# Two cross-attention stages: float32r scores on half-array row pairs, other rings of banks, transferred tail rows, and scores three steps ahead

## The reference

```
# first cross-attention: 16 heads of 16 features, 1024 context rows, a mask
qh = split(q @ wq.T + bq);  kh = split(k @ wk.T + bk);  vh = split(v @ wv.T + bv)
scores = where(mask == 0, -1e9, einsum('bhqd,bhkd->bhqk', qh, kh) / 4)
out = (softmax(scores) @ vh) @ wo.T + bo
# second: one key/value head of 16 features for all 16 query heads, 512 memory rows that are
# chosen first, row by row, by an argmax over the context
logits = einsum('bhld,bmd->bhlm', qh, mk) / 4
out = (softmax(logits) @ mv) @ Wc.T
```

## Time and profile before

| | |
|---|---|
| median of 3 timed runs | 982.57 us |
| the profiled execution, its own time | 984.73 us |
| its span, first to last instruction | 982.3 us |
| mean granted TensorE clock | 0.961 |
| PE busy, share of the span | 889.5 us, 91% |
| DVE busy | 668.3 us, 68% |
| ACT busy | 500.9 us, 51% |
| first cross-attention, first score to last values | 152.9 to 379.8 us |
| second cross-attention, the same | 716.9 to 845.9 us |

### The profile page before, as it was taken

How to read it: one execution, slowest core, us unless ns; L and a number is a source line. 1 busy time by engine, 2 the same in 40 slices (tenths; PEclk the granted TensorE clock), 3 DMA queues, 4 the chain that set the end, 5 groups by cost and what they waited for, 6 DMA issues and landing times. The chain is left out here.

```text
span 982.3 us, 13451 instructions
## 1 busy us (share of the span) xinstructions
PE 889.5 (91%) x4332; PEld 488.0 (50%) x4332; DVE 668.3 (68%) x1371; ACT 500.9 (51%) x996; POOL 334.9 (34%) x340
## 2 busy tenths in 40 slices
PE   5889988999999998599999999998989999769996
PEld 2445553433333324366667888787433322534575
DVE  4865667888889944435558776875699896455654
ACT  3786544677777773012126656563207778243321
POOL 7335636400000001136557666563420000125833
PEclk9999998999999999699989999999998999959999
DMA  5030017122212810753240000000200550075200
GB/s 157 1 139 22 1 31 117 24 51 51 48 43 53 297 54 1 261 232 126 87 129 1 1 1 1 1 1 1 81 3 20 194 196 1 1 281 181 70 17 27
DMA packets 41656, 73.81 MB, mean 75 GB/s; under 512 B 8964, under 2 KB 27780, under 8 KB 40436
## 3 DMA queue, kind: packets, MB, share of 16 engines
q1 hardware_dynamic: 36372, 59.68, 19.9%
q0 software_dynamic: 4400, 13.11, 4.3%
q10 hardware_dynamic: 816, 0.17, 0.1%
HBM read 49.67 MB, written 10.49 MB: 61 GB/s over the span
## 5 line engine op out<-in xcount | busy, mean ns | idle before, releaser
L1081 DVE TENSOR_REDUCE c_amx<-PS 128x1 f32<-128x512 f32 x256 | 159.1, 683 | 27.5 <-PE PS L981 27.1
L1174 ACT ACTIVATE c_aE<-PS 128x512 f32<-128x512 f32 x256 | 132.6, 602 | 47.1 <-PE PS L993 46.9
L1881 POOL TENSOR_SCALAR s_Pn<-s_Pr,s_rs 128x512 f32<-128x512 f32 x64 | 100.4, 1569 | 55.7 <-DVE s_rs L1923 55.6
L72 POOL TENSOR_SCALAR rstd<-mv 128x4 f32<-128x4 f32 x8 | 1.9, 234 | 336.6 <-DVE mv L95 336.6
L981 PE MATMUL PS<-c_aKs,c_aQs 99*128 99x512 bf16 x256 | 96.4, 387 | 5.1 <-DMA c_aQs<-area 3.6
L993 PE MATMUL PS<-c_aQs,c_aKs 99*128 99x512 bf16 x256 | 94.5, 380 | 3.5 <-ACT c_aE L1174 2.3
L1081 DVE TENSOR_REDUCE h_amx<-PS 128x1 f32<-128x512 f32 x128 | 79.5, 682 | 8.7 <-PE PS L981 8.3
L1174 ACT ACTIVATE h_aE<-PS 128x512 f32<-128x512 f32 x128 | 67.6, 600 | 21.6 <-PE PS L993 21.3
L2019 ACT ACTIVATE s_Pr<-PS,s_nmx 128x512 f32<-128x512 f32 x64 | 44.2, 690 | 65.5 <-DVE s_nmx L1916 65.5
L1004 PE MATMUL PS<-c_aE,c_VB 128*17 128x512 f32 x512 | 67.4, 598 | 0.1
L981 PEld LDWEIGHTS PS<-c_aKs,c_aQs 99*128 99x128 bf16 x256 | 24.9, 98 | 79.0 <-DVE c_amx L1081 55.4
(11 more groups left out here) (486 smaller groups left out, 1969.7 us busy)
## 6 DMA issues: line engine op xcount, KB each, us to landing
area<-in_e_w SPq DMA_DIRECT2D x16, 512.0 KB, 10.1
area<-in_g_w SPq DMA_DIRECT2D x8, 1024.0 KB, 6.3
c_aKs<-area SPq DMA_DIRECT2D x48, 128.0 KB
g_B<-in_g_b SPq DMA_DIRECT2D x1, 4096.0 KB, 14.1
c_aQs<-area SPq DMA_DIRECT2D x48, 64.0 KB
h_aQs<-h_QP SPq DMA_DIRECT2D x48, 64.0 KB
early<-in_ctxT SPq DMA_DIRECT2D x2, 1024.0 KB, 7.6
e_B<-in_e_b SPq DMA_DIRECT2D x1, 2048.0 KB
```

The source lines that it names most:

```text
L1081: dve.tensor_reduce(self.mx[:, qt, j, half:half + 1], PS[:, n % MB, :], AX.X, ALU.max).then_inc(self.max_done, 1)
L1174: act.activation(self.E[kt % 2][:, j, :], PS[:, MB + x % XB, :], ACT.Exp, scale=0.25).then_inc(self.exp_done, 1)
L1881: pool.tensor_scalar(Pn[g % NPB][:, :], Pr[g % NPB][:, :], rs[:, g % NPB:g % NPB + 1], None, ALU.mult).then_inc(pn_ready, 1)
```

## The change

**Operands.** Queries and keys are split into two float32r parts in place of three bf16 ones. Three blocks of 16 rows do (`NBLK` = 3), with the three tail rows ahead of them: 51 rows. They stand twice, for even heads from partition 0, for odd heads from partition 64 (`rows_of_head`), so that a product uses one half of the array's rows. The two matrices of a step's pair always use opposite halves: the second pass takes heads in the order 1, 0, 3, 2 (`x ^ 1`). The copies and subtractions that made the third part, on ScalarE, VectorE and GpSimd, go away. Bytes per unit are nearly the same: 102 rows of 2 x 1024 float32 against 99 of 4 x 1024 bf16.

**Banks.** The maxima rotate over four banks and the exponentials over three; there is no bank for transposes alone. The transposed maxima take a turn in the exponentials' ring, the transposed output one in the maxima's (`special_item`, `out_item`).

**Tail rows.** ScalarE copies the transposed maxima once, all 128 partitions, into `MTs` (`copy_maxima`), and SP sends three rows to each of four heads (`tails`). The transposes stand three steps ahead of the unit's end.

**Scores three steps ahead** (`AHEAD` = 3) and so 11 in place of 9 steps' scores ahead of the first stage's first step, 7 in place of 5 in the second.

**Loads.** SP's queue first fetches the constant query tails once into the chip (`load_tail`), and then sends them, two transfers for each unit. The second mixture's experts are loaded from ScalarE's queue, in units 1 to 4 at steps 0 and 2.

The core of the diff:

```diff
-NBLK = 6
+NBLK = 3
-MB, XB = 3, 3
+MB, XB, VALUE_BANK = 4, 3, 6
+AHEAD = 3
...
-        self.Qs = [sb(f"Qs{n}", [ROWS, GH, S], BF16) for n in range(NQ)]
-        self.Ks = [sb(f"Ks{n}", [ROWS, KH, NK], BF16) for n in range(NKB)]
+        self.Qs = [sb(f"Qs{n}", [P, PAIRS_H, S], F32R) for n in range(NQ)]
+        self.Ks = [sb(f"Ks{n}", [P, self.KP, NK], F32R) for n in range(NKB)]
...
-        n = (u + 1) * self.C + kt + 1
+        n = (u + 1) * self.C + kt + AHEAD
...
+        for u in range(UNITS):
+            self.tails(sp, u)
+            if u + 2 < UNITS:
+                if u >= 1:
+                    sp.wait_ge(self.av_done, u * self.KT)
+                load(u + 2, (u + 2) % 3)
+
+    def tails(self, sp, u):
+
+        sp.wait_ge(self.t_copied, u + 1)
+        for j in range(GH):
+            sp.dma_start(self.Qs[u % self.NQ][tail_of_head(j), j // 2, :].bitcast(F32),
+                         self.MTs[32 * j:32 * j + TAIL_ROWS, :].bitcast(F32)).then_inc(self.tails_in, 16)
...
+            item = self.max_item(u, c, j)
+            self.wait_max_bank(pe, item)
+            r = rows_of_head(j)
+            pe.matmul(self.max_bank(item), self.Qs[u % self.NQ][r, j // 2, qt * P:(qt + 1) * P],
+                      self.Ks[self.key_buffer(u)][r, j // 2 % self.KP, half * BANK:(half + 1) * BANK],
                       start=True, stop=True).then_inc(self.s_done, 1)
...
+            j = x ^ 1
+            r = rows_of_head(j)
+            if kt == 0 and x == 0:
+                pe.wait_ge(self.tails_in, 16 * GH * (u + 1))
...
-                if kt == KT - 1 and u + 1 < UNITS:
...
+                if kt == KT - AHEAD and u + 1 < UNITS:
                     maxima_transposes(u + 1)
...
-        for c in range(C + 1):
+        for c in range(C + AHEAD):
...
-        def tails(u):
+        def copy_maxima(u):
             act.wait_ge(self.mT_done, u + 1)
-            for j in range(GH // 2):
-                act.activation(self.Qs[u % self.NQ][TAIL:ROWS, j, :],
-                               PS[32 * j:32 * j + TAIL_ROWS, 7, :].bitcast(BF16)[:, 0:S],
-                               ACT.Copy).then_inc(self.q_ready, 1)
+            if u > 0:
+                act.wait_ge(self.tails_in, 16 * GH * u)
+            act.activation(self.MTs[:, :], self.exp_bank(self.special_item("m", u)).bitcast(BF16)[:, 0:S],
+                           ACT.Copy).then_inc(self.t_copied, 1)
...
-KEY_SLOTS = ((0, 3, 5), (1, 4), (2,))
-QUERY_SLOTS = ((0, 1, 2), (3, 4), (5,))
+KEY_SLOTS = ((0, 1), (2,))
+QUERY_SLOTS = ((0, 2), (1,))
...
+                if 1 <= u <= ExpertWeights.EXP // 2 and kt % 2 == 0:
+                    sh.weights[1].load_expert(act, 2 * (u - 1) + kt // 2)
```

More of the change, by code:

```diff
@@ L1140, in vector @@
         negated(0)
-        maxima(1, 0)
-        if between:
-            between()
-        upper_tails(0)
+        for c in range(AHEAD):
+            maxima(1, c)
         for u in range(UNITS):
@@ L1325 @@
     NK = 1024
-    RING = (6, 5, 3, 4, 7)
+    RING = (6, 5, 3, 4)
     FIRST = 2
@@ L1666, in late_values @@
             def late_values(act, u, kt):
-                if kt == 4 and u < UNITS // B:
-                    for t in range(KT + VLATE * u, KT + VLATE * (u + 1)):
-                        take_values(t)
+                if late_tile(u, kt) is not None:
+                    take_values(late_tile(u, kt))
             at.scalar(act, during=late_values)
@@ L2426, in _ @@
                 first_part(n)
-            for n in range(KD):
-                second_part(n)
             for k in range(KD):
```

429 lines of the change are left out of this document (215 added, 214 removed).

## The result

The changed kernel takes 1008.9 us (median of 4 runs, 1006.9 to 1010.9) against 983.4 for the kernel before on the same chip (4 runs): a ratio of 1.0259, 95% interval 1.0228 to 1.0289. It is 25.5 us slower; 961 was forecast, and the upper end of the range was 985. The profiled execution has a span of 1005.1 us and a mean granted clock of 0.932 (before: 982.3 and 0.961).

The account below looks back on a forecast made before the run. TensorE was taken to set the pace, VectorE close behind and the bound after the change. First stage 16 plus second 5.9 gave 21.9 us: 984.7 became 962.8, forecast as 961 because the profiled run lay 2.2 above the median; range 949 to 985.

Parts of the forecast that it names:

- C: Rival, pairs in both attentions: the halves do not overlap, a step is 2.93 us, 983.8 us in all; chance 0.12.
- D: Rival, pairs: no overlap and each turn between halves loses 0.10 us, a step is 3.73 us, 1046 us; chance 0.07.
- E: Rival, loops: the clock stays low as half arrays count for less, steps about 4 us, 1050 or more; chance 0.04.
- A step costs TensorE 4 x 0.25 + 0.10 + 0.99 = 2.1 us, and the pace falls to VectorE.: Attention steps: pairs, turn and values take TensorE 2.1 us, so VectorE sets 2.64 a step, 21.1 us a first-stage unit.
- The turn from pairs to values, 0.10: TensorE's step: 0.10 us over a distance is lost between the last product and the values.
- the banks hide all but about 0.6: First-stage loop: TensorE stands some 1.9 us for a unit's load, about 0.6 unhidden; five units, 3 us.
- I charge 2 us: Second stage: 2 us charged for transfers, with tail rows having 0.7 us to spare and experts' transfers beside them.
- Rival B: Turns between units wait for transfers; 17 us more if nothing hides it, 978 us; chance 0.15.
- The starts: Ahead of both loops: the first begins 5.5 us later; the second's tail rows are in by 742, hidden.
- A: The main forecast, VectorE setting the pace, with its own range 950 to 971 us; chance 0.62.

Follow-up runs that it names:

- the value order alone: Changed kernel with the value products of the step before placed ahead of the fourth pair on TensorE; 998.6 us, ratio 1.0145 to the kernel before.
- the version that won: Changed kernel with values ahead of the fourth pair, first-stage query rows issued by GpSimd, experts' loads by SyncE behind the last tail rows; 979.5 us, ratio 0.9939.
- all parts with filling products: Changed kernel with values ahead of the fourth pair, GpSimd query rows, experts' loads on SyncE, and identity products ahead of both loops; 980.1 us, ratio 0.9933.

## Why the prediction was wrong

The change does what it says. The products of a pair start together, and pairs are 0.24 us apart, against 0.25 forecast. The step of 2.62 us is below C's 2.93 and D's 3.73, and the products are back at full clock within the first steps, so rivals C, D and E fell. VectorE's 21.07 us a unit are as forecast. The errors, by the prediction's own steps:

1. **"A step costs TensorE 4 x 0.25 + 0.10 + 0.99 = 2.1 us, and the pace falls to VectorE."** This is the step that failed. The sum has no ring (buffers used in turn) in it. Three banks under the exponentials let three transposed products go, and the fourth waits for product, exponential and release: 1.22 us behind the first; with 0.42 and 0.98 that is 2.62. I had that very wait in the earlier trace rows ("the fourth waits for an exponential bank") and used it for the last steps alone. The step so came out near VectorE's 2.64, which looked like a confirmation. But a TensorE without slack pays all extras on top, 3.4 us a unit of transposes and late values: 24.4, not 21.1, as the run with GpSimd's loads shows without any halt. Against the 2.81 us of the step before, the halves gave 0.19, as much as the way to VectorE's pace (0.17), but without the slack that was to cover all extras.
2. **The turn from pairs to values, 0.10.** It is 0.42 between the last product's start and the values', over a distance of 0.24 a loss of 0.18; the earlier trace rows had 0.31 over 0.215. With the longer first product (0.49 us, 0.38 before) the last steps take 2.58 instead of 2.38. The Trainium skill (TensorEngine Tiling (Array Packing), Key Properties) has it that a change of tiling mode drains the engine; by that rule, a turn loses time, and the trace agrees (0.18 us here; in the run that spread the values, 0.43 from each pair to its value product instead of the 0.24 to the next pair).
3. **First stage, loop: "the banks hide all but about 0.6".** 16 issues took 11.4 us, not 9.7: the query tails took 0.67 us each and the key tails 0.75, where I had 0.27 for the queries' and the blocks' 0.6. The banks can't hide a halt when TensorE is the bound. It cost up to 1.95 us, with windows of clock 0.57 and 0.62 behind the two longest. But taking most of it away gave only some 2 us, within the noise (the run with GpSimd's loads).
4. **Second stage: "I charge 2 us" for transfers.** This is the mis-sized term: moving the experts' loads behind the tail rows gave 12 us (14.4 within the stage). With them the tail rows came 3.4 to 4.1 us after the last issue, not 2.4 (without them 1.2), TensorE stood for 6.7 us in three halts, and the clock was at 0.5 for 8 us behind two of them. Rival B named the mechanism, with 1.5 us for each of six units.
5. **The starts.** The first loop began 6.9 us later (5.5 forecast), with 8 us of half clock behind it, about as forecast. From the first stage's last copy to the second's first exponential it was 4.7 us more than before. The forecast has 3.9 of it: it lets the second pass begin at 742 instead of 738.09. But the stretch varies from trace to trace, from 358.9 (the value order alone) over 359.9 (the version that won) to 374.6 us (all parts with filling products), while its work is nearly the same; the last one also has the clock at half level longest, for 57 us against 45 in the changed kernel's trace and 33 in the shortest. What starts it is not shown.

Forecast were 21.9 us less in the span, measured 22.8 more: 44.7 apart. The first stage has 24.3 of them (steps 1 to 3), the second with its start 18.5 (14.4 of it step 4), the rest 1.9. The version that won is still 18 us above the forecast. Its second stage takes 97.4 us from first exponential to last copy, as forecast (742 to 839.0). Its first ends at 378.5, where 363.9 was forecast, and its unit is 23.64 us with TensorE at 23.37: step 1 stands in it. Not shown is what a full step costs with four banks in both rings; the banks don't reach for that beside the values' own, and it wasn't tried. For the full steps the chain is so read from the timelines, from the first exponential that came 0.2 us later and made the step as much longer, and from the ring of three on the other side; only for steps without scores did a fourth bank take it away (2.6 to 2.0 us).

The prediction's range for A starts at 950, where its own terms give 952.5 (961 less 8.5), and B's 1.6 us a unit would be 1.3 beyond the 0.6 already charged. Neither changes the outcome.

## What to carry to other kernels

When a change makes one engine's work shorter, write out the latency chain of each buffer ring the new step goes through (product, consumer, release) before adding up busy times: with n buffers and a group of n + 1, the chain is in every group. A step that comes out at the next engine's pace isn't thereby bound by that engine; ask which one has slack for the extras. And small transfers that are waited for want no bulk loads beside them, whichever queue the bulk is in.

## What the hardware showed that was not expected

- Float32r products on 51 of 64 rows in opposite halves overlap fully: a pair every 0.24 us. With two neighbours in the program's order on one half, TensorE started the third product, on the other half, with the first and ahead of the second (253.56 and 253.90), so the halves stayed in use together. What two products on one half cost is not shown.
- Four fp32 value products on four column strips pass in 0.98 us, one alone in 0.96.
- An issue on SyncE's queue from one on-chip tensor to another took 0.64 us for three rows and 0.59 for a block of 16 rows with 2 x 512 numbers; GpSimd's took 0.50 to 0.54.
- Tail rows of 6 KB were there 1.2 us behind the end of their last issue, and 3.4 to 4.1 us with 1 MB loads beside them.
- In the loops of the changed kernel's trace each of the five halts of 1.86 to 2.71 us was followed by 3 to 10 us at half clock (1.2 GHz); one of 0.47 us (278.80) wasn't, nor were two of at most 1.0 us in the run with GpSimd's loads. But in the trace with the experts' loads on SyncE, and in that with the value order and GpSimd's loads, the clock also fell where no wait was longer than 0.5 us.
